# An attention kernel whose five engine orders come from a build-time walk over step durations, with the weighted sum between the second and third score product of a key tile

## The reference

```python
# layer 0, per image: windows of 7 x 7, 8 heads of 8 channels
q, k, v = split(xw @ qkv_w.T + qkv_b)
qn, kn = q / norm(q), k / norm(k)
attn = softmax(qn @ kn.T * scale + bias[rel_index])
h = relu(group_norm(x + (attn @ v) @ proj_w.T + proj_b))
m = relu(w1 @ group_norm(h) + b1)
z = relu(group_norm(h + w2 @ m + b2))
# layer 1, per image: 4 heads of 16 channels over all 3136 positions
q, k, v = split(w_qkv @ z)
out = w_proj @ (softmax(q.T @ k / 4) @ v) + z
```

## Time and profile before

| | us |
|---|---|
| median of three runs | 13579.03 |
| the profiled execution, its own time | 13596.65 |
| its span | 13594.8 |
| TensorE matmuls busy | 10259.9 |
| VectorE busy | 7793.6 |
| ScalarE busy | 6665.1 |
| GpSimd busy | 2866.9 |

### The profile page before, as it was taken

One profiled execution on the slowest core, in us unless ns is written; L12 is line 12 of the kernel. 1 busy time (PEld: TensorE's weight loads), 2 busy tenths in 40 slices (PEclk: granted clock), 3 DMA queues, 4 the chain that ended last, 5 costly groups with the idle time before them and its releaser, 6 DMA issues.

```text
span 13594.8 us, 221286 instructions
## 1 busy us (share of the span) xinstructions
PE 10259.9 (75%) x69254; PEld 3810.3 (28%) x69254; DVE 7793.6 (57%) x10100; ACT 6665.1 (49%) x14018; POOL 2866.9 (21%) x786
## 2 busy tenths in 40 slices
PE   3589586895858958588585886958779586795898
PEld 1233232332323323233232322323223232332332
DVE  2366464664646646466464665646556465674675
ACT  0146354563545635356363553635546354463576
POOL 6310403104040040401304013040220403104000
PEclk9598798997979979799797988979889798997899
DMA  0101001010010200102011020110101001010010
GB/s 17 24 6 20 15 14 21 6 22 14 13 22 6 31 6 14 20 6 31 5 16 19 5 31 6 17 18 7 29 6 19 16 8 28 6 21 15 13 20 13
DMA packets 108484, 213.65 MB, mean 16 GB/s; under 512 B 52438, under 2 KB 84118, under 8 KB 107162
## 3 DMA queue, kind: packets, MB, share of 16 engines
q1 hardware_dynamic: 107298, 198.50, 9.1%
HBM read 65.75 MB, written 41.47 MB: 8 GB/s over the span
## 4 chain that ended last, share of the span: by engine, by line
PE 57%; POOL 16%; DVE 14%; issue 7%; DMA 2%; SPq 2%; ACT 1%; DVEq 0%; ACTq 0%; POOLq 0%
PE PS L1128 17%; PE PS L1117 15%; POOL tok_h L580 15%; PE PS L983 11%; DVE small L765 9%; PE PS L1024 3%; PE PS L1042 2%; DMA x_in<-in_x 2%; PE PS L1072 2%; PE PS L1080 1%; PE PS L1032 1%; DVE small L798 1%; SPq L485 1%; PE PS L1088 1%; DVE small L809 1%
## 5 line engine op out<-in xcount | busy, mean ns | idle before, releaser
L692 ACT ACTIVATE exps<-PS 128x392 f32<-128x392 f32 x12800 | 5875.0, 497 | 6455.3 <-PE PS L1117 6310.3
L765 DVE TENSOR_REDUCE small<-PS 128x1 f32<-128x784 f32 x6400 | 5934.9, 968 | 2274.1 <-PE PS L983 2268.9
L1117 PE MATMUL PS<-q_stack,k_stack 99*128 99x392 bf16 x12800 | 3879.7, 348 | 67.3 <-issue 41.7
L983 PE MATMUL PS<-k_stack,q_stack 96*128 96x392 bf16 x12800 | 3271.9, 343 | 539.8 <-DVE small L765 503.7
L1128 PE MATMUL PS<-exps,v_all 128*32 128x392 f32 x25600 | 2962.8, 536 | 4.4 <-ACT exps L692 4.4
L1117 PEld LDWEIGHTS PS<-q_stack,k_stack 99*128 99x128 bf16 x12800 | 1185.0, 99 | 3418.8 <-ACT exps L692 2448.7
L580 POOL TENSOR_TENSOR tok_h<-tok_h,vec 128x784 f32<-128x784 f32 x16 | 2003.7, 125233 | 136.0 <-DVE tok_h L786 136.0
L983 PEld LDWEIGHTS PS<-k_stack,q_stack 96*128 96x128 bf16 x12800 | 1166.9, 101 | 1667.9 <-DVE small L765 971.3
L1014 PE MATMUL PS<-tok_h,w_spread 128*128 128x392 f32 x256 | 120.0, 601 | 1989.4 <-POOL tok_h L580 1981.0
L790 DVE SCALAR_TENSOR_TENSOR tok_unit<-tok_qk,vec,PS 128x784 f32<-128x784 f32 x64 | 66.0, 1031 | 2045.1 <-PE PS L1014 2045.1
L598 POOL TENSOR_TENSOR win_scores<-win_scores,small 128x784 f32<-128x784 f32 x256 | 384.1, 1501 | 3858.3 <-DVE small L810 3858.3
(11 more groups left out here) (98 smaller groups left out, 4825.0 us busy)
## 6 DMA issues: line engine op xcount, KB each, us to landing
q_stack<-tok_qk SPq DMA_DIRECT2D x320, 98.0 KB, 3.9
k_stack<-tok_qk SPq DMA_DIRECT2D x320, 98.0 KB, 4.2
kmask<-tok_unit SPq DMA_DIRECT2D x1024, 12.2 KB
scratch_att<-o_st SPq DMA_DIRECT2D x512, 26.0 KB
att<-scratch_att SPq DMA_DIRECT2D x33, 392.0 KB
z_half<-scratch_z SPq DMA_DIRECT2D x33, 392.0 KB, 11.4
inv_sums<-scratch_rden SPq DMA_DIRECT2D x132, 98.0 KB, 3.2
out<-inv_sums SPq DMA_DIRECT2D x33, 392.0 KB, 3.7
```

The costliest lines, as they stand in the source:

```text
L692: nc.scalar.activation(exps(u), PS[:, u % SCORE_BANKS, 0:GTOK], ACT.Exp, scale=D1 ** -0.5).then_inc(s_exps, 1)
L765: nc.vector.tensor_reduce(max_parts[:, n_:n_ + 1], slot(), op=ALU.max, axis=AX.XY)\
L983: last = mm(PS[:, it.bank + j, 0:GTOK], q_stack[0:STACK, stage // 2, tile * 128:(tile + 1) * 128], k_stack[0:STACK, stage // 2, chunk * GT ...
L1117: mm(PS[:, u % SCORE_BANKS, 0:GTOK], k_stack[0:STACK + SHIFT, h, kt * 128:(kt + 1) * 128], q_stack[0:STACK + SHIFT, h, c * GTOK:(c + 1) * ...
```

## The change

One list for all engines is replaced by a table of steps, each with its parts, their engines and durations in units of 10 ns; by a table of what each step needs; and by a walk (`arrange`) that takes engine after engine and at each moment gives it the step that is ready, with the order of choice shown in the code. The engines then execute what the walk wrote down for each of them. TensorE's tile becomes: score, score, weigh, score, score, with the other items where the walk had TensorE free. The maxima may start from the first tile of a pass and go at two per tile at most. The groups of layer 0 are ten tiles apart instead of eight, and `earliest_unit()` says from which tile on a step may be taken.

Four pieces of work change too. The head sums go into one bank instead of two. The inverse norms become a square root on ScalarE and a reciprocal on VectorE, over 128 x 392 numbers. `piece_l` moves from VectorE to GpSimd. Ten more small loads of constants stand in the prologue.

```diff
+PARTS = {
+    "score": (("PE", 17),), "exp": (("ACT", 41),), "weigh": (("PE", 86),),
+    "max": (("PE", 34), ("DVE", 90)), "shift": (("PE", 25), ("DVE", 16), ("SP", 25)),
...
+    "norms": (("ACT", 310), ("DVE", 250)), "spread": (("PE", 140), ("DVE", 96)),
+    "kload": (("SP", 60),), "queries": (("SP", 8),), "twice": (("POOL", 85),),
...
+    "stack": (("SP", 90),), "vcopy": (("POOL", 60),),
+    "sums": (("SP", 16),), "zload": (("SP", 8),), "srecip": (("DVE", 36),), "rden": (("SP", 8),),
+    "rspread": (("SP", 32),), "scale": (("POOL", 370),), "final": (("PE", 140), ("DVE", 111)), "write": (("SP", 8),),
+}
+SHIFT_PIECES = 140
+TAIL = {"PE": 20, "DVE": 18, "ACT": 18, "POOL": 15, "SP": 350}
+STACK_TAIL = 900
...
+MAX_START, MAX_RATE = 1, 2.0
...
+def earliest_unit():
...
+        quad[at("qk", i)], quad[at("spread", i)] = 6 + i, 15 + i
+    first, period = 20, 10
...
+        quad[at("final", 1, k)], quad[at("final", 0, k)] = 8 + k, 185 + k
...
+def arrange(needs, maxima, attended, slot=0, last_slots=()):
...
+        path += [at("score", 4 * q + j) for j in range(2)] + ([at("weigh", q - 1)] if q else [])
+        path += [at("score", 4 * q + 2), at("score", 4 * q + 3)]
...
+    while left:
+        engine = min(ENGINES, key=lambda e: free[e])
...
+                if kind == "max":
+                    if maxima[taken] != step[1:] or unit < UNITS - 1 and taken > MAX_START + MAX_RATE * unit / 4:
+                        continue
...
+                rank = {"shift": 0, "max": 2}.get(kind, 1)
+            elif engine == "PE":
+                if path[walked] != step:
+                    continue
+                rank = 3
+            else:
+                rank = 1 if engine == "DVE" and kind not in SLOTS else 0
+            if part == 0 and unit < pace.get(step, 0):
+                continue
...
-                elif it.kind == "sum":
-                    pl.wait_ge(s_sums_bounded, t + 1)
-                    nc.gpsimd.tensor_tensor(tok_h[:, 0:PAIR], tok_h[:, 0:PAIR],
-                                            minus_half.broadcast_to([128, PAIR]), ALU.pow).then_inc(s_norms_inverted, 1)
...
+                elif it.kind == "norms":
+                    act.wait_ge(s_sums_bounded, t + 1)
+                    nc.scalar.activation(tok_h[:, 0:GTOK], tok_h[:, 0:GTOK], ACT.Sqrt).then_inc(s_norms, 1)
...
+                elif it.kind == "norms":
+                    dve.wait_ge(s_norms, t + 1)
+                    nc.vector.reciprocal(tok_h[:, 0:GTOK], tok_h[:, 0:GTOK]).then_inc(s_norms_inverted, 1)
```

More of the change, by code:

```diff
@@ L41 @@
 STAGE_MAXIMA = [[m for m in MAXIMA if m[0] == stage] for stage in range(STAGES)]
-SLOT_KINDS = ("qk", "sum", "spread", "wscore", "wtrans", "wval", "wpv", "wproj", "gn", "mlp1", "mlp2", "gqk", "gv",
-              "final", "max", "shift")
-VECTOR_SHARE = {"qk": 1.0, "sum": 1.0, "spread": 1.0, "wscore": 2.0, "wsum": 1.35, "wval": 0.7, "wproj": 1.2, "gn": 0.4,
-                "mlp2": 1.2, "hstats": 1.15, "rest": 1.0, "piece_l": 1.0, "gv": 0.7, "final": 1.2, "max": 1.0}
-def layer0():
-    at = []
-    def put(when, kind, i=0, j=0):
-        at.append((when, len(at), (kind, i, j)))
+LEAD = 6
@@ L57, in layer0, with at, all_of, layer0_needs @@
+LEAD_IN = STAGE_MAXIMA[0] + STAGE_MAXIMA[1][:LEAD]
+Step = namedtuple("Step", "kind i j k")
+Entry = namedtuple("Entry", "kind i j k part bank")
+def at(kind, i=0, j=0, k=0):
+    return Step(kind, i, j, k)
+def all_of(kind, count):
+    return [at(kind, n) for n in range(count)]
+def layer0_needs(attended):
+    needs = {}
+    def step(this, *before):
+        needs[this] = [b if isinstance(b, tuple) and not isinstance(b, Step) else (b, None) for b in before]
     for g in range(GROUPS):
-        put(1 + 0.8 * g, "xload", g)
@@ L208 @@
-PROLOGUE, MORE, LAST = prologue_plan(), image_plan(True), image_plan(False)
-assert sum(item.kind in SLOT_KINDS for quad in MORE for part in quad for item in part) % 2 == 0
-EPILOGUE = with_banks([item for _, item in finish_half(1, 0)])
+            quad[at("wscore", g, half)], quad[at("wtrans", g, half)] = base + 1.5 * half, base + 5 + 1.5 * half
+        quad[at("wval", g)], quad[at("wpv", g)], quad[at("wproj", g)] = base + 3, base + 8.5, base + 10
+    done = first + period * (GROUPS - 1) + 13
```

474 lines of the change are left out of this document (257 added, 217 removed).

## The result

| | median us | lowest to highest |
|---|---|---|
| before (4 runs beside it) | 13598.13 | 13576.19 to 13633.13 |
| changed | 10922.52 | 10901.71 to 10960.80 |

The ratio is 0.8034, with a 95% interval from 0.8003 to 0.8064: a fifth faster. The profiled execution took 10960.8 us, with a span of 10959.0.

A forecast was written before the change was run, and what follows sets the result against it. No engine was full; GpSimd's power, which TensorE's `spread` waits for, was taken to stop the core 123.8 us a pass. Prologue 400 + 15 passes x 660 + last pass 541 = 10841, forecast 10840 us, range 10100 to 11500.

The forecast's parts named there:

- The power's price and place: GpSimd's element-wise power ahead of `spread` stops the whole core; replacing it takes 123.8 us off a pass.
- The tables: Two table loads a pass on ScalarE, 1.28 us each; with the square root counted at 3 us a pass.
- The start: Pass start: loads of x behind z hold `qk` to +27.5 and `sum`'s end to +52; 18 us a pass lost.
- The mixed stretches: Where layer 0 lies between tiles: of 111 us lost before, a third, 38 us a pass, remains.
- Half 0's end and stage 6: Half 0's closing DMA chain comes 5 us late; stage 6's shift behind two `stack` steps costs 3 us.
- The weighted sum's place: In each tile the weighted sum follows two scores, not three; it fits by 0.07 us, costed at nothing.
- The last pass: The pass without layer 0: 519 + 13 (late first `final`) + 5 + 4 = 541 us.
- The prologue: Before the first pass: 524 - 125 + 7 + 5 - 11 = 400 us.
- The sum: Whole kernel: prologue 400 + 15 passes x 660 + last pass 541 = 10841 us.
- The rival that the clock stays low: TensorE's clock falls at pass starts and stays low: slower than before, some 17700 us if low throughout; chance 0.02.
- The rival "as planned": New order works, x loads not held up behind z, few slot waits: 613 us a pass, 10115 in all; chance 0.24.

The follow-up runs named there:

- the base: The changed kernel run once more, unaltered, beside the follow-up runs: 10917.19 us (0.8033).
- the two runs: Each the changed kernel with one edit: copy ahead of maxima in VectorE's choice, 10735.83 us; ScalarE's `relu`, `mlp_in` and `zrelu` each a tile apart, 10760.07 us.
- the last two experiments: The changed kernel with the four alterations, 10407.22 us; the same with the weighted sum back behind the third score, 10638.39 us.
- the four alterations: The changed kernel with the pass start rearranged, half 0's z early, copy ahead of maxima, relus apart (only partly there): 10407.22 us (0.765).

## Why the prediction was right, and where it was off

- **The power's price and place**: right. 2670 us were gained; the norms alone, in the old order, give 1940 (16 x 123.8 = 1981 less the new chain). The reciprocal took 2.59 us (forecast 2.6), the square root 0.53 (0.46).
- **The tables**: 2 x 1.28 us, and the next instruction begins 0.02 us behind a load. The Trainium skill's 2.66 us per switch ("ScalarE: Activation LUTs", What ACT_TABLE_LOAD costs) would have been too much; by the trace, the load is all there is here.
- **The start**: right in place and mechanism, and right in size with some luck. In the ten short passes `sum` ended at +49 to +53 for my +52, and tiles 0 to 20 took 81 us for 84.6. The five passes with 34 to 38 us at the lower clock, for which my sum has no term, bring the mean to 84.7. The 18 us a pass weren't all idle time either: up to tile 20 TensorE stood idle for 10 to 13 us, and ran at the lower level for 19 to 23 us in the short passes. Moving the loads of x gave 10.9 us back. I had not seen VectorE's wait for the sums, but that wait brought nothing when it was taken away by itself.
- **The mixed stretches**: I kept a third of the loss, 38 us; 427.5 us for tiles 20 to 140 against my 423.8 make it 42. The size was a choice, and its cause was not the one I gave. I blamed VectorE's bunches of layer 0. The runs show 12 us of it in the walk's bunches of maxima ahead of the copy and 10 in ScalarE's relus (means of tiles 20 to 140: 426.9 in the base, 414.5 and 417.1 in the two runs). The other 20 have no run. Nor has any run shown what took the 57 us that the new order gained there.
- **Half 0's end and stage 6** (5 + 3): the terms that were too small. Tiles 140 to 200 took 158.9 for 151.5. I counted the late time alone; the trace has 5.8 us of waiting and 14 us at a clock of 0.67 around and behind it. Stage 6's shift cost next to nothing: all scores together waited 10.7 us for shifts in the whole run.
- **The weighted sum's place**: costed at nothing, and that is what the clean tiles show, 2.24 us with either place (before and changed). The 231 us between the last two experiments aren't its price: they go with where the walk put the pairs of maxima and one `shift`. In the stretches with layer 0 TensorE does wait for ScalarE at the weighted sum (98.7 us in the whole run, 4.4 before); with the sum behind the third score about as much shows at scores and maxima.
- **The last pass**: its first `final` came 30 us in (forecast 32), tiles 0 to 20 were 12.9 us longer (forecast 13), but tiles 20 to 180 took 362.1 us for 374.3. That gain isn't the sum's place. The kernel before had 17 tiles of 2.5 to 4.0 us there, at the ends of stages and between them; the changed one has none above 2.6. I had looked at one clean tile only. So the pass grew by 8 us instead of 22; the other 6 lie in my split of before, where the count gives its last pass 513 and not 519 (its first was 849).
- **The prologue**: -32 us. I had guessed 11 for closer groups; all that lies behind the first `spread` gave 45 (first `spread` to first score, 305.5 us before and 260.3 now).
- **The sum**: -32 + 15 x 11.15 (167) + 3 (pass 1) - 20 = +118 us of 10841. Errors of both signs, none above 1.6%.
- **The rival that the clock stays low** came in small. Behind half 0's end the clock was back at 1.00 in the next window, with TensorE busy all the time. The Trainium skill's rule that activity lifts the throttle ("TensorE: Matmul & The Clock Gate", Part 1) agrees with that window, but not with the 37.5 us at 0.50 in pass 5, in which TensorE was just as busy. Five such stretches cost 10 to 14 us each, some 60 us in all. For the 42 us of the kernel before I had written that TensorE had work all the time; it was busy for 38.6 of them, and its longest wait was 2.94 us.
- **The rival "as planned"** (613 a pass; its total adds up to 10136 and not 10115): with the four alterations a pass comes to 636, about halfway between it and my 660.

## What to carry to other kernels

Before replacing a slow instruction, ask whether its user can stand further behind: the same power cost 805 us in one order and 43 in another. An order from a walk is as good as its table and its choices: one rank that let maxima starve a copy cost 181 us, and shows in the trace as a wait at the same tile of every pass. Judge an edit to such a walk by stretches, not by the total, since it moves everything else too: the sum's place read as -0.4% in one order and +2.2% in another, and neither number was the price of the place. Look into the combined kernel as well: an alteration that worked alone can be gone there.

## What was not expected of the hardware

Waits that add up to as much can cost less. Four waits of 0.72 us, about 3 us apart, left TensorE at full rate; one of 2.62 us was followed by a product at nearly twice its time (1.54 for 0.87 us), and one of 2.29 us by 13.7 us at the lower clock. At the start of a pass, behind the wait for x, the clock stayed low for 14 us at the most in ten passes and for 34 to 38 us in five, with TensorE busy for all but about 1 us of them. What sets that, no run shows. A transfer's price to others is not its issue: z took 0.55 us to issue; the store of the inverses behind it was ready for the next step after 9.9 us, and after 6.6 without z.
